# Loading the first half of the attention's output inside the attention, and moving the wait for its last stores

## What is computed

```
x = x + 0.5 * ffn(layernorm(x))        # this one, "rope" and "ffn0" in the kernel
x = x + linear_attention(layernorm(x))
x = x + 0.5 * ffn(layernorm(x))        # the same function and weights again
x = x + 0.5 * moe(x)                   # "ffn1"
x = x + causal_attention(x)            # "causal"
x = x + 0.5 * moe(x)                   # "ffn1" again

def ffn(src):
    q, k, v = src @ Wq, src @ Wk_c @ Wk, src @ Wv_c @ Wv     # 16 heads of 8
    q, k = rope(q), rope(k)
    sa = softmax(q k^T / sqrt(8)) @ v @ Wo
    x = rmsnorm(src + sa, norm1_w)
    out = x + swiglu(x @ W_shared_in) @ W_shared_out + top-2 of 8 experts, weighted
    return rmsnorm(out, norm2_w)
```

## Time and profile before

| | |
|---|---|
| median of three runs | 4322.61 us (4318.81 to 4332.14) |
| the profiled execution's own time | 4312.76 us |
| its span, first to last instruction | 4310.6 us |
| mean granted TensorE clock | 0.923 of full speed |
| busy: PE, DVE, ACT, POOL | 3664.0, 3126.4, 2000.5, 1187.6 us |
| first pass of attention ends, output projection begins | 828 to 842 us of the span |
| second pass: the same | 2279 to 2292 us of the span |

### The profile page before, as it was taken

The page is one execution under the profiler, slowest core; times in us unless marked ns, Lnnn a source line. Parts: engine busy times, 40 slices in busy tenths (PEclk is TensorE's granted clock), DMA queues, the critical chain, the costliest instruction groups (busy, mean ns, idle before and its releaser), DMA issues. The chain is left out here.

```text
span 4310.6 us, 59958 instructions
## 1 busy us (share of the span) xinstructions
PE 3664.0 (85%) x20847; PEld 1626.9 (38%) x20847; DVE 3126.4 (73%) x7330; ACT 2000.5 (46%) x2982; POOL 1187.6 (28%) x1186
## 2 busy tenths in 40 slices
PE   6999999889789789999997874548999999998464
PEld 2222222254344422222224444544444444443464
DVE  7999999366666799999974664356767767765434
ACT  2677777521344337777773112323444444443132
POOL 1000000010312100000000114434666666666533
PEclk8999999999899879999998986778999999999587
DMA  4111111200300041111112012330000000000233
GB/s 119 56 54 52 49 52 50 91 25 1 105 1 1 24 106 49 52 52 54 53 38 100 1 46 73 87 90 2 2 2 2 2 2 2 2 2 17 83 100 93
DMA packets 326956, 192.82 MB, mean 45 GB/s; under 512 B 168606, under 2 KB 282066, under 8 KB 326658
## 3 DMA queue, kind: packets, MB, share of 16 engines
q1 hardware_dynamic: 310594, 155.14, 13.4%
q0 software_dynamic: 14336, 33.58, 2.7%
q10 hardware_dynamic: 1728, 0.28, 0.0%
HBM read 119.74 MB, written 67.90 MB: 44 GB/s over the span
## 5 line engine op out<-in xcount | busy, mean ns | idle before, releaser
L774 DVE TENSOR_REDUCE ra_mh<-PS 128x1 f32<-128x512 f32 x2048 | 1300.1, 683 | 21.3 <-PE PS L640 9.6
L722 ACT ACTIVATE ra_p<-PS 128x1024 f32<-128x1024 f32 x1024 | 994.2, 1021 | 436.4 <-PE PS L648 436.0
L657 PE MATMUL PS<-ra_p,ra_va 128*32 128x512 f32 x4096 | 563.8, 605 | 0.3
L648 PE MATMUL PS<-ra_q,ra_k 75*128 75x512 bf16 x2048 | 537.2, 383 | 3.8 <-ACT ra_p L722 1.5
L610 POOL DMA_DIRECT2D o_heads<-rp_rot x128 | 67.4, 531 | 1482.7 <-ACT rp_rot L730 1482.7
L2336 ACT ACTIVATE ca_p<-PS 128x1024 f32<-128x1024 f32 (+3 forms) x384 | 304.8, 811 | 357.9 <-PE PS L2235 355.9
L2386 POOL TENSOR_TENSOR ca_s<-ca_s,ca_p 128x1024 f32<-128x1024 f32 (+3 forms) x256 | 412.3, 1611 | 75.4 <-ACT ca_p L2336 54.8
L640 PE MATMUL PS<-ra_ko,ra_qo 48*128 48x512 bf16 x1024 | 408.0, 398 | 24.1 <-DVE ra_mh L774 24.1
L640 PE MATMUL PS<-ra_k,ra_q 48*128 48x512 bf16 x1024 | 407.1, 398 | 16.6 <-DMA ra_qo<-q_parts 16.0
L640 PEld LDWEIGHTS PS<-ra_k,ra_q 48*128 48x128 bf16 x1024 | 94.9, 93 | 656.0 <-DVE ra_mh L774 537.4
L2231 PE MATMUL PS<-ca_q,ca_k 64*128 64x512 f32 (+3 forms) x1536 | 318.5, 495 | 0.0
(11 more groups left out here) (261 smaller groups left out, 5582.2 us busy)
## 6 DMA issues: line engine op xcount, KB each, us to landing
ra_k<-k_parts SPq DMA_DIRECT2D x128, 144.0 KB
ra_q<-q_parts SPq DMA_DIRECT2D x128, 144.0 KB
o_heads<-rp_rot POOLq DMA_DIRECT2D x128, 128.0 KB
ao_ot<-o_heads SPq DMA_DIRECT2D x16, 1024.0 KB
f_xg<-expert_tokens SPq DMA_DIRECT2D x56, 256.0 KB, 3.3
expert_outputs<-f_yb SPq DMA_DIRECT2D x56, 256.0 KB, 2.1
expert_tokens<-X SPq DMA_DIRECT2D x28, 256.0 KB, 3.7
q_parts<-rp_parts SPq DMA_DIRECT2D x48, 128.0 KB, 2.4
```

What stands on the lines that cost most here:

```text
L648: mm = pe.matmul(PS[:, j, :], K[0:KROWS, ub, j, (step % KT) * P:(step % KT + 1) * P], Q[0:KROWS, ub, j, (step // KT) * BT:(step // KT + 1) ...
L657: mm = pe.matmul(PS[VW * j:VW * (j + 1), 4, :], VA[:, ub, step % KT, j, :], PR[:, s % 2, j, :], start=(s % KT == 0), stop=(s % KT == KT - ...
L722: act.activation(PR[:, s % 2, PH * pair:PH * (pair + 1), :], PS[:, PH * pair:PH * (pair + 1), :], ACT.Exp, scale=float(DH) ** -0.5).then_i ...
L774: dve.tensor_reduce(mh[:, pair, KT * odd + t, h:h + 1], PS[:, bank, :], AX.X, ALU.max).then_inc(s_max, 1)
```

## The change

A new class `Output` owns the tile `ao_ot`, its four load semaphores, and the two semaphores that count the attention's stores. It is made before `rope` and lives until `ffn0` ends. `Output.load` is the old load of one block; `Output.stored(sp, b)` lets SP wait until the stores that sequence b needs have landed. The attention's SP stream, after its last `max_rows`, waits for `s_low` and for the stores of sequences 0 and 1, and loads blocks 0 to 3. POOL no longer waits for its stores. In `ffn0` SP begins with the experts' weights; before blocks 4 and 6 it waits for the stores of sequences 2 and 3. To make room in SBUF, `t`, `qk` and `res` become views of `ao_ot`.

```diff
-        rope(nc, a, g)
-        ffn0(nc, a, g)
+        rope_and_experts(nc, a, g)
...
+class Output:
+    HELD = 4
+
+    def __init__(self, g, sb, sem):
+        self.O = g["O"]
+        self.ot = sb("ao_ot", [P, self.HELD, NG, BT])
+        self.s_ot = [sem(f"ao_o_loaded{u}") for u in range(self.HELD)]
+        self.s_os = [sem(f"ra_o_stored{h}") for h in range(2)]
+
+    def load(self, sp, n):
+        b, u = divmod(n, 2)
+        sp.dma_start(self.ot[:, n % self.HELD, :, :], self.O[NG * b + 1:NG * (b + 1) + 1, :, u * BT:(u + 1) * BT].rearrange(
+            "g p s -> p g s")).then_inc(self.s_ot[n % self.HELD], 16)
+
+    def stored(self, sp, b):
+        stores = NG * (b + 1) + 1
+        for h in range(2):
+            sp.wait_ge(self.s_os[h], 32 * min(stores, BATCH * NG))
...
-        self.t = sb("rp_t", [P, 2, 2, 2, BT])
-        self.qk = sb("rp_qk", [P, 2, 2, BT])
-        self.res = sb("rp_res", [P, 2, 2, BT])
+        self.t = room[:, 0:8, :].rearrange("p (u h k) s -> p u h k s", u=2, h=2)
+        self.qk = room[:, 8:12, :].rearrange("p (u k) s -> p u k s", u=2)
+        self.res = room[:, 12:16, :].rearrange("p (u k) s -> p u k s", u=2)
...
+            sp.wait_ge(project.s_low, NBLK)
+            for b in range(output_rows.HELD // 2):
+                output_rows.stored(sp, b)
+                for n in (2 * b, 2 * b + 1):
+                    output_rows.load(sp, n)
             for pair in range(2):
                 for u in range(2):
                     sp.wait_ge(s_mr[pair][u], 16 * PARTS * ITERS // 2)
...
             store(ITERS, 1, (1,))
-            pool.wait_ge(s_os[0], 32 * ITERS)
-            pool.wait_ge(s_os[1], 32 * ITERS)
...
                 def heads(n):
-                    b, u = divmod(n, 2)
-                    if n >= HELD:
-                        sp.wait_ge(s_o, n - HELD + 1)
-                    sp.dma_start(ot[:, n % HELD, :, :], O[NG * b + 1:NG * (b + 1) + 1, :, u * BT:(u + 1) * BT].rearrange(
-                        "g p s -> p g s")).then_inc(s_ot[n % HELD], 16)
-
-                for n in range(HELD):
-                    heads(n)
+                    if n % 2 == 0:
+                        output.stored(sp, n // 2)
+                    sp.wait_ge(s_o, n - HELD + 1)
+                    output.load(sp, n)
```

More of the change, by code:

```diff
@@ L231, in scalar, with rope_and_experts, rope @@
         act.wait_ge(self.copied, self.COPIES)
-def rope(nc, a, g):
+class Output:
[13 more added lines that the diff above has]
+            sp.wait_ge(self.s_os[h], 32 * min(stores, BATCH * NG))
+def rope_and_experts(nc, a, g):
+    with ExitStack() as ctx:
+        output = Output(g, *stage(nc, ctx))
+        rope(nc, a, g, output)
+        ffn0(nc, a, g, output)
+def rope(nc, a, g, output):
     with ExitStack() as ctx:
@@ L245, in rope, with __init__ @@
         )
-        project = Projection(a, g, sb, sem, buffers)
-        rope_attention(nc, g, buffers, sb, sem, project)
+        project = Projection(a, g, sb, sem, buffers, output.ot)
+        rope_attention(nc, g, buffers, sb, sem, project, output)
 class Projection:
     HELD = 4
-    def __init__(self, a, g, sb, sem, buffers):
+    def __init__(self, a, g, sb, sem, buffers, room):
         self.a, self.g, self.buffers = a, g, buffers
+        room = room[:, :, :, :].rearrange("p a b s -> p (a b) s")
         self.ln = LayerNorm(g, sb, sem)
@@ L469, in scalar, with rope_attention @@
         mid(NBLK - 1)
-def rope_attention(nc, g, buffers, sb, sem, project):
+def rope_attention(nc, g, buffers, sb, sem, project, output_rows):
     IDN, PS, QQ, KK, V, O = (g[k] for k in ("IDN", "PS", "QQ", "KK", "V", "O"))
@@ L537, in rope_attention @@
     s_exp = [sem(f"ra_exp_done{p}") for p in range(2)]
-    s_os = [sem(f"ra_o_stored{h}") for h in range(2)]
+    s_os = output_rows.s_os
     s_va, s_tile, s_max, s_mx, s_mp, s_pv, s_of, s_ch = (
@@ L813, in top2, with ffn0 @@
         ch.link(dve.scalar_tensor_tensor(w, rank, 1.5, p, ALU.is_lt, ALU.mult))
-def ffn0(nc, a, g):
-    X, XN, XNT, IDN, PS, PW, O = (g[k] for k in ("X", "XN", "XNT", "IDN", "PS", "PW", "O"))
+def ffn0(nc, a, g, output):
+    X, XN, XNT, IDN, PS, PW = (g[k] for k in ("X", "XN", "XNT", "IDN", "PS", "PW"))
+    ot, s_ot, HELD = output.ot, output.s_ot, output.HELD
     G = GA + E0
-    HELD = 4
     FT = HID // P
@@ L840, in ffn0 @@
         n1 = sb("ao_n1", [P, D])
-        ot = sb("ao_ot", [P, HELD, NG, BT])
         rc = sb("ao_rc", [P, 2, TPB * H0])
@@ L872, in ffn0 @@
         z = sb("e0_z", [P, TPB, D])
-        s_ot = [sem(f"ao_o_loaded{u}") for u in range(HELD)]
         s_ew = sem("ao_experts_weights")
```

## The result

The changed kernel takes 4306.74 us (median of 11 runs), the kernel before 4321.91 us (11 runs beside it): ratio 0.9969, 95% interval 0.9959 to 0.9978. In two later series, beside the same kernel before, the ratio was 0.9966 (0.9954 to 0.9978) and 0.9971 (0.9961 to 0.9981). The medians lie 13.0 to 15.9 us apart. The forecast was 4308.3 us, which is 14.3 us less, from a median of 4322.61 us for the kernel before.

A forecast was written before the change was run, and what follows sets the result against it. PE idles 14.42 us at the attention's end behind the last store, POOL's closing and the first load. Gains of 5.2 + 1.6 + 0.4 and 5.2 + 1.6 + 0.3, together 14.3 us, from 4322.61 give 4308.3 us; range 4301 to 4317.

The forecast's parts named there:

- The first four loads: Attention's end: loads issued behind the last row maxima leave the path to PE's first transposes; 5.2 us gained per pass.
- The last store's landing: Attention's end: POOL enters its closing at the last issue, not the landing; 1.6 us gained per pass.
- Rival 1: POOL's closing starts with the store's landing, so 2 x 1.6 us are not gained: 4311.5 us; chance 0.20.
- rival 2: POOL's closing with a transfer in the air is dearer, at most 10.29 us from last issue: 4317.0 us; chance 0.05.
- Block 4 no longer late: Output projection in ffn0: block 4's load comes sooner and PE's waits vanish; 0.4 and 0.3 us gained.
- ACT's six small loads: Before project of block 0: wait for these loads between 0 and 2.4 us, taken as 0.
- the third rival: ACT's small loads bind PE's first project, 2.4 us in each pass: 4313.1 us; chance 0.13.
- The clock: Behind PE's earlier start: the clock stays at 1.2 GHz for the same 8.5 us, so the stage moves whole.
- Rival 4: The clock stays low longer behind PE's new start, 7.6 us slower per pass: 4337.8 us; chance 0.04.

The follow-up runs named there:

- preload_only: The changed kernel with POOL's two waits for its stores put back; 4306.74 us, ratio 0.9976 to the kernel before.
- stores_split: The changed kernel with each of POOL's stores cut into two halves of its columns; 4312.51 us, ratio 0.9992 to the kernel before.
- sp_stores: The changed kernel with all 64 attention stores per pass issued by SP instead of POOL; 4080.25 us, ratio 0.9941 to the kernel before.
- pool_free: The changed kernel with its first four loads back at the beginning of ffn0, POOL still not waiting; 4314.95 us, ratio 1.0000 to the kernel before.
- small_early: The changed kernel with the six small loads issued by SP in the attention, behind the heads; 4085.23 us, ratio 0.9951 to the kernel before.
- after_again: The changed kernel, unchanged, run and traced again; 4301.02 us, ratio 0.9966 to the kernel before.
- after_again2: The changed kernel, unchanged, once more in series 3; 4302.63 us, ratio 0.9971 to the kernel before.
- Series 2: Four changed kernels run on a chip of its own beside the kernel before, which took 4105.02 us there.

## Why the prediction was right, step by step

**The first four loads, 5.2 us per pass: right.** preload_only measures 5.3. They were issued at 796.28, right behind the last `max_rows`, PE's start follows the block's by 0.2 us, and the attention was not slowed: from the start of POOL's first store issue to the end of its last it takes 686.5 us (142.54 to 829.01 before, 147.26 to 833.74 now). The two stores among them took 5.7 us from issue to landing, and nobody waited.

**The last store's landing, 1.6 us per pass: right, and slightly small.** It is 1.9 to 2.0 us: from 7.53 to 5.56 behind the last issue, and 7.49 with the wait put back. Rival 1 (the closing starts with the landing) would have left the block's start 7.5 us behind the issue, and rival 2 would have put it near 10. Both fall. The reason I gave, that the closing is work for each DMA issued, was an argument from two rows; stores_split and sp_stores bear it out: 0.95 and 0.66 us in the two passes without POOL DMAs, 5.56 with 64, 10.8 with 128.

**Block 4 no longer late, 0.4 and 0.3 us: right.** The wait is gone in both passes. pool_free shows that the term carries more than its size: there block 4 did not come sooner by as much as PE, and the 1.9 and 1.7 us gained at PE's start were lost. Whether the larger gain of the full change would have been lost without it was not run.

**ACT's six small loads at 0 us: wrong.** This is the step of the forecast that failed, by the third rival's mechanism. PE's idle time before the first `project` was 3.07, 3.14, 1.59, 1.17, 2.74 and 0.71 us in three profiles of the changed kernel, of which 0.69 is ACT's copy. The extra is 0 to 2.45 us, 1.4 on average; small_early gets 1.1 of it back. I had put it at 0, because 4.2 MB of heads no longer ran beside them. But the small loads now share the DMA engines with the weights and with block 4. Two of the other rows, after_again first and then after_again2's second pass:

```profile
848.50 1.13 PE L963 MATMUL PS<-ao_wo,ao_saT 128*128 128x128 f32 x8 [1.59 <-DMA ao_n<-in_L_ffn_norm_w]
2293.27 1.14 PE L963 MATMUL PS<-ao_wo,ao_saT 128*128 128x128 f32 x8 [0.71 <-ACT ao_saT L1203]
```

The loads are not what differs between these passes. In all six the last of their packets has run 9.7 to 10.1 us behind the block's start, and `project` begins 10.4 to 10.8 us behind it. What differs is when PE is ready: 8.0 to 8.4 us behind the start in the three passes with the long waits, 9.9 to 10.5 in the others. The forecast had PE ready after 10.05 us, so with its own clock the wait would have been under 1 us. The DMA view of the changed kernel, 839 to 848 us:

```profile
q1 hardware_dynamic: 1632, 1.15, 41.2%
q10 hardware_dynamic: 830, 0.13, 7.9%
```

By then 830 of ACT's 864 packets have run, 8.7 us behind the block's start. The Trainium skill, page "DMA: Bandwidth & Descriptors", section "Queues, rings and completion order", says that each DMA engine takes turns between the queues with work, a packet at a time. The trace does not contradict this, but it does not single it out: the last small packet has run 9.7 us behind the start beside 1.5 MB on SP's queue, and 11.6 us behind it before, beside 3.0 MB (the forecast took 12.5 us, the end of its window). Half the bytes beside them brought the small loads 1.9 us sooner, and no run had them on an otherwise empty queue, so how much of the 9.7 us is SP's doing is not known.

**The clock, the same 8.5 us at the lower level: right in half of the passes.** Windows of the changed kernel's first pass, from the block's start on:

```profile
839.30:842.30 3.00, 2.82 (x14) 2.85 (x15) 0.00 (x0) 0.00 (x0) 0.00 (x0) 0.50 0.14 41
842.30:849.10 6.80, 2.87 (x24) 2.43 (x23) 2.50 (x4) 0.60 (x1) 0.00 (x0) 1.00 0.77 225
849.10:852.60 3.50, 2.88 (x14) 2.92 (x14) 0.69 (x1) 0.07 (x1) 0.00 (x0) 0.51 1.10 355
```

The clock rose within the first step, at 842.3, and fell again from 849.1 to 852.6; PE had been waiting for the small loads since 846.65. Its second pass and after_again2's first went the same way. In the other three passes the clock rose 8.3 to 9.5 us behind PE's start, near the 8.5 assumed, and did not fall again. With the early rise PE is ready sooner and so waits longer for the small loads. The early rise gained nothing in the end: the way to block 7 is 43.5 to 43.8 us with it and 42.6 to 42.9 without. Rival 4 did not come.

**The sum.** 14.3 us were forecast. The way to block 7 gives 2 x 6.7 = 13.4 us, the medians 12.97 to 15.87. The term that failed, the small loads, is 2 to 3 us of the whole, and the store's term was 0.7 us too small. So the forecast came as near as it did in part because these two errors have opposite signs. The price for reading the total of one profile would have been higher: the profile of the changed kernel was 3.3 us longer than that of before.

## What to carry to other kernels

An engine's own closing after its DMAs can stand on the path at a block's end though no row is busy there. Count the DMAs that POOL issues in a block, and issue them on another queue where a barrier follows soon: here that was worth more than taking the wait away (3.0 us per pass with the small loads in the way, against 1.9). When a pause is shortened, look at the transfers just behind it: they have to come sooner too, or the wait only moves, and takes the clock down with it. Measure a small change by the stretch that it touches, from an event just before it to one just behind.

## What the hardware showed that I had not expected

**POOL's closing costs some 0.08 us for each DMA.** That is an estimate from three kernels: (10.79 - 5.56) / 64 = 0.082 us, and (5.56 - 0.95) / 64 = 0.072. It begins at the last issue, not at the landing. Whether it depends on the time since the DMAs were issued, and what POOL does in it, was not tried. An issue on SP's queue took 0.45 us and one on POOL's 0.53 in these rows. The Trainium skill, page "DMA: Bandwidth & Descriptors", section "SWDGE vs HWDGE vs iDMA", says that GpSimd's descriptors are made by software and the others' by hardware with less set-up. In these rows the issues differ by 0.08 us, and the closing adds about as much again for each DMA of POOL's; that second part no other queue showed.

**The same kernel takes 5% less on another chip.** Series 2 has 4105 us for the kernel before, the others 4316 to 4322. The attention takes 686.5 us there too. From the second attention's last issue to the last gather of the first `ffn1` after_again takes 593.7 us and small_early 488.8. The groups of one of its lines, first in after_again, then in small_early (series 2), over windows that hold the whole of that stage (2340 to 2870 and 2340 to 2850):

```profile
L1822 PE MATMUL PS<-f_xT,f_wb 128*128 128x128 f32 x480 | 75.3, 308 | 71.5 <-issue 58.5 <-DVE f_wb L1994 10.3 <-ACT f_hh L1881 1.7
```

```profile
L1829 PE MATMUL PS<-f_xT,f_wb 128*128 128x128 f32 x480 | 65.4, 281 | 3.5 <-DVE f_wb L2001 3.2
```

58.5 us in which PE waited for nothing that the profile shows are absent on the other chip. They are about half of the 105 us. Their cause was not looked for.

**The first attention's start.** In the five profiles of kernels with loads in the attention and 64 stores on POOL (the changed kernel three times, preload_only, small_early), the clock stays low for 48 to 55 us from 81 on, and POOL's last issue ends at 831.1 to 833.7. In the nine others it is 44 us, and 828.4 to 830.4. Windows of the changed kernel, and of before:

```profile
123.00:135.70 12.70, 12.70 (x36) 1.95 (x35) 8.26 (x14) 3.08 (x3) 0.00 (x0) 0.50 0.00 1
```

```profile
123.50:135.70 12.20, 11.60 (x47) 2.75 (x47) 12.03 (x25) 4.94 (x5) 0.00 (x0) 1.00 0.00 1
```

The five end the attention 2.9 us later than the nine on average, and all of it arises before the attention's first store. pool_free has the same instructions up to 790 us and does not show it, so the change's code in that stretch is not the cause. It can be chance, since the clock's changes come at other times of the span in every execution, or something that goes with the program as a whole. Whether the runs without a profile have it too is unknown. If they did, 10.5 of the 13.4 us would be left. The medians of 13.0 to 15.9 us speak against it, but 10.5 us lie inside all three intervals. This stays open.
